# Quantised attention by head pairs: separate memory for the second batch's norm parts, a first score after two projections, projections in other steps and banks

## What is computed

```
def make_fxp(x):
    x = clip(x, -(8 - 1/4096), 8 - 1/4096)
    return trunc(x * 4096) / 4096
h = layernorm(x)                          # per position, no weights
q, k, v = make_fxp(h @ w_qkv)             # 16 heads of 64 features
score = make_fxp(q @ k.T / 8)
attn = make_fxp(softmax(score))
out = make_fxp(attn @ v)
x = x + make_fxp(out @ w_proj + b_proj)
```

## Time and profile before

| | us |
|---|---|
| median of 3 runs | 1752.82 |
| lowest and highest | 1752.27, 1757.22 |
| the profiled execution | 1751.54 |
| its span | 1750.2 |

### The profile page before, as it was taken

One profiled execution on the slowest core, in us unless ns is written; L12 is line 12 of the kernel. 1 busy time (PEld: TensorE's weight loads), 2 busy tenths in 40 slices (PEclk: granted clock), 3 DMA queues, 4 the chain that ended last, 5 costly groups with the idle time before them and its releaser, 6 DMA issues. The chain is left out here.

```text
span 1750.2 us, 22355 instructions
## 1 busy us (share of the span) xinstructions
PE 1612.3 (92%) x7513; PEld 824.6 (47%) x7513; DVE 1038.3 (59%) x2138; ACT 902.7 (52%) x1740; POOL 432.7 (25%) x545
## 2 busy tenths in 40 slices
PE   7999998999999789999997989999988989999997
PEld 3344444345666344444333555555433445455545
DVE  5732026483314668888855888888548716565515
ACT  2531214243334557777845778888533754555513
POOL 1000100000000145555511556555301102233300
PEclk9999999999999999999998999999998999999999
DMA  6000100001000000000025321111137202000000
GB/s 232 0 1 0 43 0 1 36 0 72 1 1 19 0 10 19 11 10 10 29 97 194 119 82 39 45 28 28 33 70 232 60 1 100 12 22 12 1 0 25
DMA packets 36888, 74.11 MB, mean 42 GB/s; under 512 B 4460, under 2 KB 23404, under 8 KB 35340
## 3 DMA queue, kind: packets, MB, share of 16 engines
q1 hardware_dynamic: 36774, 72.68, 13.0%
HBM read 55.79 MB, written 16.78 MB: 41 GB/s over the span
## 5 line engine op out<-in xcount | busy, mean ns | idle before, releaser
L2496 POOL TENSOR_TENSOR work<-work,arena_b 128x512 f32<-128x512 f32 x128 | 167.7, 1311 | 123.5 <-ACT work L2358 123.5
L2448 DVE CUSTOM_DVE_ANT_0 work<-ps,arena_a 128x1024 f32<-128x1024 f32 x128 | 154.6, 1209 | 0.0
L2340 ACT ACTIVATE work<-work,small 128x1024 f32<-128x1024 f32 x128 | 146.6, 1145 | 4.3 <-DVE small L2448 4.2
L2242 PE MATMUL ps<-identity,work 128*128 128x128 f32 x1024 | 139.8, 278 | 9.0 <-ACT work L2358 4.8
L2242 PEld LDWEIGHTS ps<-identity,work 128*128 128x128 f32 x1024 | 116.0, 143 | 57.3 <-issue 29.8
L3348 POOL TENSOR_SCALAR ctx_keys<-ctx_keys,small 128x128 f32<-128x128 f32 (+3 forms) x128 | 67.0, 537 | 172.5 <-DVE small L3271 172.5
L2460 DVE TENSOR_TENSOR work<-ps,arena_b 128x512 f32<-128x512 f32 x128 | 88.0, 687 | 35.0 <-PE ps L2242 33.0
L2358 ACT ACTIVATE work<-ps 128x512 f32<-128x512 f32 x128 | 76.2, 595 | 60.3 <-PE ps L2242 57.4
L2018 POOL TENSOR_SCALAR work<-work 128x1024 f32<-128x1024 int32 x64 | 66.6, 1041 | 112.7 <-DVE work L1971 112.2
L2231 PE MATMUL ps<-work 96*128 96x512 bf16 x256 | 79.7, 395 | 11.6 <-DVE small L2448 7.7
L1804 PE MATMUL ps<-work 64*128 64x512 f32 x256 | 72.5, 642 | 16.7 <-DVE work L1971 14.6
(11 more groups left out here) (405 smaller groups left out, 3383.9 us busy)
## 6 DMA issues: line engine op xcount, KB each, us to landing
work<-parts_k_L_xattn SPq DMA_DIRECT2D x14, 384.0 KB, 4.0
arena_a<-in_mask SPq DMA_DIRECT2D x2, 2048.0 KB, 7.7
arena_b<-in_groupT SPq DMA_DIRECT2D x2, 2048.0 KB, 9.7
head_weights<-in_w_L_xattn SPq DMA_DIRECT2D x8, 449.0 KB, 3.2
arena_a<-in_w_l_attn SPq DMA_DIRECT2D x1, 3072.0 KB, 14.4
head_weights<-in_w_L_attn SPq DMA_DIRECT2D x8, 384.0 KB, 3.1
work<-parts_q_L_attn SPq DMA_DIRECT2D x8, 384.0 KB, 4.5
work<-parts_k_L_attn SPq DMA_DIRECT2D x8, 384.0 KB, 5.4
```

The costliest lines, as they stand in the source:

```text
L2242: mm = pe.transpose(t_psum[z][:, kt * P:(kt + 1) * P], prob[i % NP][:, o:o + P], k.iden[:, :])
L2340: act.activation(p, p, ACT.Exp, scale=-1.0, bias=minmax[:, i % 8:i % 8 + 1], accum_out=sums[:, i % 8:i % 8 + 1]).then_inc(*exped.up())
L2448: dve.tensor_tensor_reduce(prob[i % NP], s_psum[i % NS], NEG[:, b, qt, :], -1.0, BIG * 3e8, OP.add, OP.min, minmax[:, i % 8:i % 8 + 1]).th ...
L2496: pool.tensor_tensor(p, p, GT[:, b, 4:8, qt * P:(qt + 1) * P], OP.mult).then_inc(*weighed_pool.up())
```

## The change

The second batch's `sq` and `tmp` get memory of their own, in what later holds the signs of the scores (`sign`, whose first use comes after both scalings); the norm parts of both batches are issued batch by batch without waiting for each other. Of the 30 beats 3 stay. The chunks of group 0 move to steps -3 to 1 and 3 (q, k, q, k, v, v); for the other groups k of batch 0, q and k of batch 1 move from steps 3, 4, 5 to 4, 5, 6 of the group before, while q of batch 0 (step 2) and v (steps 0 and 1 of the own group) stay. The first score of a group waits for q and k of batch 0 only, the first one of batch 1 for the rest. While no output product is running yet (the first ten chunks, `PAIR`), chunks take banks 7 and 6 in turn, the second one bank 4, and wait for the chunk two before. GpSimd scales the weights of group 1 right behind those of group 0.

```diff
--- before.py
+++ after.py
@@ -1745,14 +1745,16 @@
     N = G * per
     unit = lambda i: (i // per, i % per // nk, i % nk)
 
-    CHUNKS = [(0, what, n, at) for what, n, at in (("q", 0, -6), ("k", 0, -5), ("q", 1, -4), ("k", 1, -3))]
-    for g in range(G):
-        CHUNKS += [(g, "v", n, per * g + n) for n in range(B)]
-        if g + 1 < G:
-            CHUNKS += [(g + 1, what, n, per * g + at) for what, n, at in
-                       (("q", 0, 2), ("k", 0, 3), ("q", 1, 4), ("k", 1, 5))]
+    NAMES = [("q", 0), ("k", 0), ("q", 1), ("k", 1), ("v", 0), ("v", 1)]
+    CHUNKS = [(0, what, n, at) for (what, n), at in zip(NAMES, (-3, -2, -1, 0, 1, 3))]
+    for g in range(1, G):
+        CHUNKS += [(g, what, n, per * (g - 1) + at) for (what, n), at in zip(NAMES, (2, 4, 5, 6, per, per + 1))]
+    CHUNKS.sort(key=lambda ch: ch[3])
     chunk_at = {at: x for x, (_, _, _, at) in enumerate(CHUNKS)}
     made = lambda g, what: max(x for x, ch in enumerate(CHUNKS) if ch[0] == g and ch[1] in what) + 1
+    first_made = lambda g: max(x for x, ch in enumerate(CHUNKS) if ch[0] == g and ch[1] in "qk" and ch[2] == 0) + 1
+    PAIR = sum(at < per for _, _, _, at in CHUNKS)
+    c_bank = lambda x: k.bank(4 if x == 1 else 6 if x < PAIR and x % 2 else 7)
 
     ln, nxt = k.ln, k.next
     if nxt:
@@ -1766,6 +1768,7 @@
     w_scaled, q_clipped, part_fixed, clipped, summed, out_put = k.signals("pool", 6)
     masks = Masks(k) if nxt else None
     FINAL = (7, 0, 1, 2)
+    ln.sq[1], ln.tmp[1], ln.shared = view(w, 9 * K, DC, S), view(w, 10 * K, S), False
 
     def sync(sp):
         for g in range(2, G):
@@ -1787,15 +1790,23 @@
             mm.then_inc(*final.up())
 
     def tensor(pe):
-        ln.open_tensor(pe)
-        k.beat(ln.spare, 10)
+        if ln.early < 1:
+            ln.mean(pe, 0)
+        if not ln.second:
+            ln.mean(pe, 1)
+        if ln.early < 2:
+            ln.var(pe, 0)
+        ln.var(pe, 1)
+        k.beat(ln.spare, 3)
         pe.wait_ge(*ready(3))
-        for step in range(-6, N + 10):
+        for step in range(-3, N + 10):
             i = step
             if 0 <= i < N:
                 g, b, qt = unit(i)
                 s, q0 = g % 2, b * S + qt * P
                 if i % per == 0:
+                    pe.wait_ge(*part_fixed(first_made(g)))
+                elif i % per == nk:
                     pe.wait_ge(*part_fixed(made(g, "qk")))
                 if i >= 2:
                     pe.wait_ge(*truncated(i - 1))
@@ -1835,23 +1846,21 @@
                 pe.wait_ge(*w_scaled(g + 1))
                 if g == 0 and what != "v":
                     pe.wait_ge(*ln.out(n + 1))
-                if x:
-                    if step < 0:
-                        k.beat(ln.spare, 5)
+                if x >= PAIR:
                     pe.wait_ge(*part_int(x))
+                elif x >= 2:
+                    pe.wait_ge(*part_int(x - 1))
                 if what == "v":
                     for j in range(4):
                         for c in range(DC):
                             k0 = n * S + j * P
-                            mm = pe.matmul(p_bank[:, j * P:(j + 1) * P], k.Hn[:, c, k0:k0 + P], W[g % 2][2][:, c, :],
+                            mm = pe.matmul(c_bank(x)[:, j * P:(j + 1) * P], k.Hn[:, c, k0:k0 + P], W[g % 2][2][:, c, :],
                                            start=c == 0, stop=c == 1)
                 else:
                     for c in range(DC):
-                        mm = pe.matmul(p_bank, W[g % 2][what == "k"][:, c, :], k.Hn[:, c, half(n)], start=c == 0,
+                        mm = pe.matmul(c_bank(x), W[g % 2][what == "k"][:, c, :], k.Hn[:, c, half(n)], start=c == 0,
                                        stop=c == 1)
                 mm.then_inc(*part.up())
-            if step == -5:
-                ln.var(pe, 1)
             if N <= step < N + G:
                 g = step - N
                 if g == 0:
@@ -1876,9 +1885,14 @@
             nxt.mean(pe, 1, resid(2))
 
     def scalar(act):
-        ln.open_scalar(act)
+        if ln.early < 1:
+            ln.square(act, 0)
+        ln.square(act, 1)
+        if ln.early < 2:
+            ln.root(act, 0)
+        ln.root(act, 1)
         act.wait_ge(*ready(3))
-        for step in range(-6, N + 12):
+        for step in range(-2, N + 12):
             i = step - 3
             if 0 <= i < N:
                 act.wait_ge(*clipped(i + 1))
@@ -1893,9 +1907,7 @@
                 act.wait_ge(*part(x + 1))
                 if x >= 2:
                     act.wait_ge(*part_int(x - 1))
-                act.activation(psign[x % 2], p_bank, ACT.Sign).then_inc(*part_sign.up())
-            if step == -5:
-                ln.root(act, 1)
+                act.activation(psign[x % 2], c_bank(x), ACT.Sign).then_inc(*part_sign.up())
             i = step - 1
             if 0 <= i < N:
                 act.wait_ge(*scored(i + 1))
@@ -1933,14 +1945,19 @@
             nxt.root(act, 0)
 
     def vector(dve):
+        if ln.early < 1:
+            ln.centre(dve, 0)
+        ln.centre(dve, 1)
         dve.memset(back, -float(OFFSET) / FX).then_inc(*ready.up())
         dve.tensor_copy(iden16, k.iden[:, :]).then_inc(*ready.up())
         col = VCOL["L2_attn_b_proj"]
         dve.tensor_scalar(b_fx, k.vec[:, col:col + 2], FX, None, OP.mult).then_inc(*ready.up())
+        if ln.early < 2:
+            ln.scale(dve, 0)
+        ln.scale(dve, 1)
         if nxt:
             masks.bias(dve)
-        ln.open_vector(dve)
-        for step in range(-6, N + 12):
+        for step in range(-2, N + 12):
             i = step - 4
             if 0 <= i < N:
                 dve.wait_ge(*summed(i + 1))
@@ -1959,10 +1976,8 @@
                 dve.wait_ge(*part_sign(x + 1))
                 if x >= 2:
                     dve.wait_ge(*part_fixed(x - 1))
-                dve.scalar_tensor_tensor(out=pint[x % 2], in0=psign[x % 2], scalar=-HALF, in1=p_bank, op0=OP.mult,
+                dve.scalar_tensor_tensor(out=pint[x % 2], in0=psign[x % 2], scalar=-HALF, in1=c_bank(x), op0=OP.mult,
                                          op1=OP.add).then_inc(*part_int.up())
-            if step == -5:
-                ln.scale(dve, 1)
             i = step - 1
             if 0 <= i < N:
                 dve.wait_ge(*signed(i + 1))
@@ -2006,8 +2021,8 @@
 
     def gpsimd(pool):
         for step in range(-7, N + 13):
-            if step == -7 or (step >= 0 and step % per == 0 and step // per + 1 < G):
-                g = step // per + 1
+            if step < -5 or (step >= per and step % per == 0 and step // per + 1 < G):
+                g = step + 7 if step < 0 else step // per + 1
                 pool.wait_ge(*w_in[g % 2](g // 2 + 1))
                 pool.tensor_scalar(weights[g % 2], weights[g % 2], FX, 0.0, OP.mult, OP.add).then_inc(*w_scaled.up())
             i = step - 2
```

## The result

The changed kernel took 1732.51 us in the median of four runs (1729.97 to 1733.78), the kernel before 1755.02 in that session; the ratio is 0.9866, with a 95% interval of 0.9837 to 0.9896. The forecast was 1729.5, faster. Medians here are over all executions of a session, while the ratios leave out four that lasted far longer (3566 us in `after_again`, 2820 in `all_four`, 4058 in `no_beats`, 1921 in the kernel before).

A forecast was written before the change was run, and what follows sets the result against it. The prediction took TensorE to set the pace, VectorE close behind, with a serial chain at the start. Gains of 16.3 and 7.0 made 23.3, so span 1728.2, plus 1.3 for the median: 1729.5 us, range 1724.5 to 1738.

The forecast's parts named there:

- The start: From the quantised attention's release to its first score: first score at 607.4 instead of 620.61, 13.2 us earlier.
- The filling: Steps 0 to 15, VectorE the bound from step 4: step 16 at 665.7 instead of 682.04, gain up to there 16.3.
- The steady groups: Groups 2 to 6: moved projections shorten the period from 33.83 to 32.42, 1.4 us per group, 7.0 for five.
- The unknown cost: VectorE's normalising in step 7: taken as nothing at 0.88 us; at 1.69 about 0.35 a group, 2.1 over six.
- The sum: Whole stage: 16.3 up to step 16 plus 7.0 from the groups, 23.3 us, giving a time of 1729.5.
- Rival A: VectorE becomes the bound of the steady groups; only 16.3 us remain, 1736.5; chance 0.14.
- Rival B: The clock falls in the filling, one more dip elsewhere: some 6 us lost, 1735.5; chance 0.13.
- Rival C: Half clock from the stage's release to step 8: 7 to 10 us slower, 1760; chance 0.03.
- Rival D: Old waits and steady stall stay, or later stages eat the gain: within 5 of before, 1749; chance 0.04.

The follow-up runs named there:

- after_again: The changed kernel run once more with the same code in a second session: 1729.91 us, ratio 0.9854 to the kernel before.
- all_four: The changed kernel, but from group 1 on a group's first score waits for all four clipped q and k: 1758.66 us, ratio 1.0031.
- no_beats: The kernel before with 3 instead of 30 beats in this stage and nothing else: 1756.80 us, ratio 1.0015.
- exp_later: The changed kernel with ScalarE's two exponentials issued behind the signs in steps 3 and 7 of a group: 1732.43 us, ratio 0.9867.
- exp_step3: The changed kernel with ScalarE's exponentials behind the signs in step 3 of a group only: 1730.86 us, ratio 0.9866.
- shared_norm: The changed kernel with one norm buffer for both batches, in the same order of issue: 1732.77 us, ratio 0.9883.
- one_bank: The changed kernel with all projections in bank 7 again, each waiting for the rounding of the one before: 1736.67 us.

## Why the prediction was right, step by step

- **The start.** First score 13.4 us earlier (24.31 to 10.89); forecast 13.2. The steps on the way: second variance at 598.69 (598.7), q0 at 601.35 (601.4), first score at 607.13 (607.4). What is left is the projections' spacing: ScalarE's sign of k0 started 1.66 behind that of q0 (605.06 and 603.40), where I had 1.92 between projections.
- **The filling.** Step 8 at 633.22 (633.5). Step 16 was earlier than forecast, 664.65 instead of 665.7, so the gain up to there was 17.4 (682.04 to 664.65), not 16.3. Of the error of 1.05, 0.3 stood at step 8 already; 0.47 is the term for steps 8 to 11, where I added VectorE's longer cases one by one (3.8, 4.2, 4.2, 3.5; measured 3.51, 4.11, 4.13, 3.48); and 0.4 is a slip in my addition: from 633.5 my own terms, 15.7 and 16.1, lead to 665.3. Steps 12 to 15 took 16.2.
- **The steady groups.** 1.17 us per group, 5.85 for five; forecast 1.4 and 7.0. The mechanism held: step 6 takes 3.46, the wait of 1.24 is gone, and ScalarE's chain of 5.77 moved to step 7 unchanged, as `exp_later` confirms by taking it apart. The mis-sized term is the score behind that chain: I took 1.27 from rounding to score, in the changed kernel it is 1.36 (695.95 to 697.31). That makes 3.68 and 3.67 for steps 3 and 7 instead of 3.58, and step 4 behind it takes 4.59 instead of 4.54.
- **The unknown cost** was nothing, as taken: the normalising in step 7 lasts 0.88 in the line of 694.12, with GpSimd idle or at its small scaling of the sums (L2037). `exp_later` shows the other side, 1.91 beside GpSimd's work; the Trainium skill, "GPSIMD Engine Reference", section 1, has the two engines share SBUF interfaces, and these numbers go with it.
- **The sum** for the stage was 23.3 and it came out at 23.2, because the two errors of about 1.1 went against each other, which is luck. The measured 1732.51 lies 3.0 above the forecast, within the range: not for anything in the stage, but in what lies behind it, which the forecast had as unchanged and which moves by several us from execution to execution.
- **Rival A** did not come: VectorE is busy 30.3 of 32.66, and the period is TensorE's 32.40 plus what ScalarE's chain adds in steps 3 and 7.
- **Rival B** is a real mechanism in the wrong place. No half clock at the start of the changed kernel, and none in the whole stage in its two profiled executions, but in five of eight executions with the same idle one lies in steps 8 to 10. The prediction says that my schedule has no such idle; that step was wrong. One of 1.94 us stands ahead of score 8, which waits for VectorE while step 7 has no projection, and it follows from my own times. It costs 1.4: in `exp_step3` steps 8, 9, 10 take 5.12, 3.52, 4.46, in the changed kernel 3.51, 4.11, 4.13, a sum of 13.10 against 11.75. Behind the stage, where the result's own profile lost up to 5.5, lies the rival's other part.
- **Rival C** did not come. The mechanism is real for the old start: the profiled execution of `no_beats` lost 6.6 us to it. I had argued against it from the clock of 1.00 with "more idle" in the start; that idle was covered by beats, so the row did not speak for the case without them. What spoke against it is in rival B's lines: my start leaves TensorE almost no idle. That this is what kept the clock up is not shown, since `one_bank` kept it with more.
- **Rival D** did not come: `shared_norm` and `one_bank`, which bring back one old wait each, cost 0.8 and 3.1 us before the first score, so in the changed kernel neither wait was left, and the period fell as forecast.

## What to carry to other kernels

Read one period of the bounding engine as start-to-start steps, find which step has idle time and which has a moved piece of work that could fill it, and check the floor that the fuller queues of the other engines set there: it moves with the pattern and can be read from the step that already has it. What an instruction needs and what stands ahead of it in its queue are two things; both count (`one_bank`, `all_four`). Filler work could be removed where real work took its place back to back, and cost up to 6.6 us where it was removed from a start with long waits; where the border lies was not found, so try both, the edit with and the old kernel without it.

## What had not been expected of the hardware

- The same code differs by 5.5 us behind the stage between executions (879.32 and 873.85), with the granted clock 0.88 against 0.90 over the 90 us of the cross attention. A single profile is not enough for differences of that size; the stage's own time repeats within 0.03 us.
- Half clock fell behind an idle of TensorE of only 1.93 us in five of eight executions, and not in the other three; in one execution of `all_four` it fell behind five of seven longer idles. What tips it was not found.
- VectorE's normalising of the same two tiles took from 0.88 to 1.91 us in these profiles, the longer the more GpSimd worked beside it: 0.88 with at most 0.5 us of GpSimd's work, 1.24 with 0.9 to 1.2, 1.66 to 1.91 with 1.25 to 1.9, a clip of a score among it.
